# An RWKV-7 layer with a mixture of experts on one core: matmuls that nobody reads, and placing tables of their own for the first and the last chunks

## The reference

```python
x = x + attn(layernorm(x))          # RWKV-7 time mixing with 16 heads of 8, then a squared-ReLU FFN
x = x + ffn(layernorm(x))           # router, top-1 of 4 experts 128 -> 512 (gelu), 512 -> 128, layernorm

def step(state, inp):               # inside attn: 512 steps, each needs the one before
    r_t, d_t, k_t, v_t, a_t, b_t = inp
    sa = einsum('bhij,bhj->bhi', state, a_t)
    state = state * d_t[:, :, None, :] + sa[..., None] * b_t[:, :, None, :] + v_t[..., None] * k_t[:, :, None, :]
    return (state, einsum('bhij,bhj->bhi', state, r_t))
```

## Time and profile before

| | |
|---|---|
| median of the runs | 1217.21 us |
| profiled execution, its own time | 1216.56 us |
| its span in the trace | 1214.7 us |
| mean granted TensorE clock | 0.931 of 2.4 GHz |
| PE busy | 1043.4 us, 86% |
| PEld busy | 566.0 us, 47% |
| DVE busy | 890.9 us, 73% |
| ACT busy | 668.6 us, 55% |
| POOL busy | 629.7 us, 52% |
| first scan step (L843) | 50.86 us |
| last scan step | 1129.38 us |

### The profile page before, as it was taken

The page is one execution under the profiler, slowest core; times in us unless marked ns, Lnnn a source line. Parts: engine busy times, 40 slices in busy tenths (PEclk is TensorE's granted clock), DMA queues, the critical chain, the costliest instruction groups (busy, mean ns, idle before and its releaser), DMA issues.

```text
span 1214.7 us, 17920 instructions
## 1 busy us (share of the span) xinstructions
PE 1043.4 (86%) x5395; PEld 566.0 (47%) x5395; DVE 890.9 (73%) x2283; ACT 668.6 (55%) x1093; POOL 629.7 (52%) x885
## 2 busy tenths in 40 slices
PE   3666689989898989989898989999798989888866
PEld 2343354455454455455454555455454545454432
DVE  4567777887878787877878787887878787876220
ACT  2634464847475565747475665847475565734331
POOL 0346565565555565555555565555555565555100
PEclk8869899999898999989998999999998999989778
DMA  3101011111111121101111121111111121100110
GB/s 123 27 9 32 21 35 27 27 36 35 44 23 48 27 53 28 35 27 35 44 25 49 25 52 28 34 29 36 44 25 47 27 53 27 38 7 22 31 26 17
DMA packets 62759, 41.88 MB, mean 34 GB/s; under 512 B 7100, under 2 KB 56252, under 8 KB 62536
## 3 DMA queue, kind: packets, MB, share of 16 engines
q1 hardware_dynamic: 62664, 40.74, 13.7%
HBM read 11.35 MB, written 4.19 MB: 13 GB/s over the span
## 4 chain that ended last, share of the span: by engine, by line
PE 58%; DVE 14%; ACT 13%; issue 7%; DMA 4%; SPq 3%; ACTq 0%; DVEq 0%
PE fin_a L514 9%; PE fin_b L514 9%; PE sa_ps L359 9%; PE pre_a L298 6%; PE mid_ps L468 5%; PE fin_b L523 3%; DVE state L857 3%; SPq L262 3%; DMA rs_f<-row_ers 3%; PE mid_ps L298 3%; DVE upd L853 3%; PE vb_ps L338 3%; ACT hid L718 2%; DVE s_a L843 2%; ACT L548 2%
## 5 line engine op out<-in xcount | busy, mean ns | idle before, releaser
L1030 POOL TENSOR_TENSOR plus_kv<-state,kv 128x128 f32<-128x128 f32 x512 | 284.7, 556 | 418.5 <-DVE state L857 393.3
L359 PEld LDWEIGHTS sa_ps<-s_a,con 128*128 128x128 f32 x1024 | 183.6, 201 | 307.2 <-DVE s_a L843 230.3
L359 PE MATMUL sa_ps<-s_a,con 128*128 128x128 f32 x1024 | 237.5, 316 | 76.0 <-DVE s_a L843 75.9
L853 DVE TENSOR_TENSOR upd<-sa_ps,b_t 128x128 f32<-128x128 f32 x512 | 147.8, 289 | 169.5 <-PE sa_ps L359 164.8
L1022 POOL TENSOR_TENSOR s_r<-state,r_t 128x256 f32<-128x256 f32 x256 | 219.1, 856 | 1.3 <-DVE state L857 1.3
L857 DVE TENSOR_TENSOR state<-upd,plus_kv 128x128 f32<-128x128 f32 x512 | 175.2, 342 | 18.0
L843 DVE TENSOR_TENSOR s_a<-state,a_t 128x128 f32<-128x128 f32 x512 | 149.4, 292 | 18.5
L548 ACT ACT_TABLE_LOAD x101 | 129.6, 1283 | 1.8
L514 PE MATMUL fin_b<-h_e,mat 128*128 128x512 f32 x256 | 128.2, 616 | 0.8 <-ACT pick L733 0.8
L514 PE MATMUL fin_a<-h_e,mat 128*128 128x512 f32 x256 | 122.1, 593 | 0.0
L830 DVE TENSOR_TENSOR kv<-vb_ps,k_t 128x512 f32<-128x512 f32 x128 | 87.5, 684 | 0.3 <-issue 0.2
(11 more groups left out here) (197 smaller groups left out, 1733.9 us busy)
## 6 DMA issues: line engine op xcount, KB each, us to landing
rs_p<-row_rs SPq DMA_DIRECT2D x128, 64.0 KB, 2.1
x_in<-xT SPq DMA_DIRECT2D x16, 256.0 KB, 3.1
rs_p<-row_rk SPq DMA_DIRECT2D x64, 64.0 KB, 2.4
x_res<-xT SPq DMA_DIRECT2D x16, 256.0 KB, 2.9
rs_m<-row_frs SPq DMA_DIRECT2D x64, 64.0 KB, 2.1
rs_f<-row_ers SPq DMA_DIRECT2D x64, 64.0 KB, 2.1
rs_f<-row_lrs SPq DMA_DIRECT2D x64, 64.0 KB, 2.1
outT<-res SPq DMA_DIRECT2D x16, 256.0 KB, 2.3
```

The lines of the kernel that those rows point to most:

```text
L359: mm(sa_ps[:, 0:STATE], k("sum8"), s_a[:], start=True, stop=True).then_inc(s["sa"], 1)
L853: tt(ib(upd[:]), ib(sa_ps[:, 0:STATE]), over_i(b_t[c.slot][:, t * B:(t + 1) * B]), ALU.mult).then_inc(s["upd"], 1)
L1030: tt(plus_kv[:, (t % 2) * STATE:(t % 2 + 1) * STATE], st(t), kv[:, at:at + STATE], ALU.add).then_inc(s["plus_kv"], 1)
```

## The change

PE gets matmuls that nobody reads. They multiply 256 columns of the constants (128x256, f32) by the weights that the scan uses, and write columns 256 to 511 of the bank `sa_ps`, of which the scan uses only the first 128. Their slots are the list `keep`. Each first waits until DVE has formed `upd` of the scan step in which it stands, so that it never writes while DVE reads the bank. In iteration -1 there is no wait, and in iterations 16 and 17 the wait is for the last `upd` of all.

There are three tables now: `AT_FIRST` for chunks 0 and 1, with 37 unread matmuls per chunk, `AT_LAST` for chunks 14 and 15 with 26, and `AT` for the other twelve with 10; 246 in all. `AT` itself moves a few operations. All other edits write the sizes of a chunk in a general form (`SIZES`, `c.n`, `c.quarters`, `values_of`); as all 16 sizes are 32, they give the same instructions as before. The scan, the arithmetic and the DMAs are the same.

```diff
+        self.place = AT_FIRST if at < 2 else AT_LAST if at >= CHUNKS - 2 else AT
...
-                if at == AT["c0"]:
+                if at == c.place["c0"]:
...
+                    sums(c, fin_b, 0, "mean32", sq_f, "lj")
+                for n in range(len(c.place["keep"])):
+                    if at == c.place["keep"][n]:
+                        now = c + at // SLOTS
+                        if now.at >= 0:
+                            pe.wait_ge(s["upd"], now.step(at % SLOTS // now.slots + 1 if now.has() else 0))
+                        mm(sa_ps[:, 2 * STATE:4 * STATE], k("sum8"), con[:, 0:2 * STATE], start=True, stop=True, skip_group_check=True)
```

`AT` in full, and of `AT_FIRST` and `AT_LAST` the lines that matter below:

```diff
 AT = {
-    "c0": -32, "j0": -31, "sq0": -31, "rs0": -28, "x_in": -24, "xh0": -23, "x1": -22, "c1": -22, "sq1": -22,
-    "rs1": -22, "j1": -21, "xn": -19, "d_rs0": -18, "xh1": -17, "wa": -16, "dx": -16, "d_rs1": -15,
-    "mix_k": -15, "k": -15, "mix_g": -15, "th_w": -15, "mix_r": -15, "mix_v": -14, "w2": -14, "key": -14,
-    "th_d": -14, "rk": -14, "kks": -13, "val_tm": -11, "v": -11, "k2": -11, "cum": -10, "g1": -10,
-    "d_rk": -10, "p": -8, "val": -8, "k_t": -7, "kk": -7, "val_sb": -6, "r": -6, "kki": -5, "rkb": -5,
-    "rec": -4, "rkb_ps": -4, "r_t": -3, "b_t": -3, "a_t": -2, "g2": -2, "th_g": -1, "bonus": 0, "gate": 0,
-    "bonus_b": 23, "x_res": 34, "gj": 37, "gsq": 37, "grs": 38, "gxh": 39, "gaff": 39, "gg": 39, "wo": 41,
-    "x2": 42, "fsq": 42, "fc": 43, "x2x": 43, "frs": 44, "fj": 45, "xf": 46, "fxh": 48,
-    "hid": (50, 51, 53, 56), "kf": 51, "d_frs": 51, "f1": (52, 52, 53, 54), "f2": (55, 56, 57, 57),
-    "d_ers": 57, "y1": 58, "ec": 58, "ej": 58, "esq": 59, "h": 61, "router": 61, "ers": 62, "best": 62,
-    "onehot": 63, "masks": 63, "h_e": (65, 66, 69, 70), "pick": 66, "pick_sb": 66,
-    "moe": (68, 68, 70, 70, 70, 71, 71, 72, 73, 76, 76, 77, 78, 78, 79, 79), "act": (70, 71, 77, 77),
-    "y1b": 78, "mo": (80, 80, 81, 82), "lsq": 84, "y2": 85, "lrs": 85, "lj": 86, "d_lrs": 86, "store": 89,
-    "lxh": 91, "res": 91,
+    "c0": -32, "j0": -30, "sq0": -30, "rs0": -29, "xh0": -23, "x1": -23, "c1": -22, "sq1": -22, "rs1": -22,
+    "x_in": -21, "j1": -21, "xn": -19, "d_rs0": -17, "xh1": -17, "d_rs1": -17, "wa": -16, "dx": -16,
+    "mix_k": -15, "k": -15, "mix_g": -15, "mix_r": -15, "th_w": -14, "mix_v": -14, "w2": -14, "key": -14,
+    "th_d": -14, "rk": -14, "kks": -13, "val_tm": -11, "v": -11, "k2": -11, "d_rk": -11, "cum": -10,
+    "g1": -10, "p": -8, "val": -8, "k_t": -7, "kk": -6, "val_sb": -6, "r": -6, "kki": -5, "rkb": -5,
+    "keep": (-5, -4, 1, 2, 28, 30, 61, 90, 92, 95), "rec": -4, "rkb_ps": -4, "r_t": -3, "b_t": -3, "a_t": -2,
+    "g2": -2, "th_g": -1, "bonus": 0, "gate": 0, "bonus_b": 23, "gj": 37, "gsq": 37, "grs": 38, "gxh": 39,
+    "gaff": 39, "gg": 39, "wo": 41, "x2": 42, "x_res": 43, "fsq": 43, "fc": 44, "x2x": 44, "frs": 44,
+    "fj": 45, "xf": 46, "fxh": 48, "d_frs": 50, "kf": 51, "hid": (52, 53, 53, 57), "f1": (52, 52, 53, 54),
+    "f2": (55, 56, 57, 57), "d_ers": 57, "y1": 58, "ec": 58, "ej": 58, "esq": 59, "ers": 59, "h": 61,
+    "router": 61, "best": 62, "onehot": 63, "masks": 63, "h_e": (65, 66, 69, 70), "pick": 66, "pick_sb": 66,
+    "moe": (68, 68, 70, 70, 71, 71, 71, 72, 73, 76, 76, 77, 78, 78, 79, 79), "act": (70, 72, 76, 77),
+    "y1b": 75, "mo": (80, 81, 81, 82), "lsq": 84, "y2": 85, "lrs": 85, "d_lrs": 85, "lj": 86, "lxh": 90,
+    "res": 90, "store": 91,
+}
+AT_FIRST = {
+    "c0": -32, "j0": -31, "sq0": -31, "rs0": -30,
+    "keep": (-28, -28, -27, -27, -25, -19, -19, -18, -15, -12, -12, -9, -7, -5, -5, -4, -1, 0, 2, 6, 7, 11, 12, 18, 22, 25, 28, 30, 33, 34, 59, 60, 63, 65, 80, 92, 95),
+    "x1": -26, "xh0": -24, "c1": -23, "sq1": -23, "rs1": -23, "j1": -22, "xn": -22, "x_in": -21, "th_w": -20,
+    "xh1": -18, "d_rs0": -17, "wa": -16, "dx": -16, "mix_k": -15, "k": -15, "mix_g": -15, "mix_r": -15,
...
+AT_LAST = {
...
+    "keep": (-4, -2, 0, 1, 2, 3, 24, 27, 29, 29, 34, 46, 54, 58, 59, 62, 82, 87, 90, 90, 91, 92, 93, 93, 95, 95),
...
+    "ej": 58, "d_ers": 61, "h": 62, "router": 62, "esq": 63, "best": 63, "ers": 64, "onehot": 64,
+    "h_e": (64, 65, 67, 69), "masks": 67, "pick": 68, "pick_sb": 68,
+    "moe": (69, 70, 70, 71, 71, 72, 74, 74, 77, 77, 80, 80, 80, 80, 81, 81), "act": (73, 74, 78, 79),
+    "y1b": 77, "mo": (81, 81, 81, 82), "lsq": 81, "lrs": 85, "d_lrs": 85, "y2": 86, "lj": 86, "lxh": 90,
...
```

More of the change, by code:

```diff
@@ new lines @@
+    "router": 61, "best": 62, "onehot": 63, "masks": 63, "h_e": (65, 66, 69, 70), "pick": 66, "pick_sb": 66,
[8 more added lines that the diff above has]
+    "xh1": -18, "d_rs0": -17, "wa": -16, "dx": -16, "mix_k": -15, "k": -15, "mix_g": -15, "mix_r": -15,
+    "key": -15, "mix_v": -14, "w2": -14, "th_d": -14, "rk": -13, "kks": -13, "val_tm": -12, "v": -12,
+    "d_rs1": -11, "k2": -11, "d_rk": -11, "p": -11, "cum": -10, "g1": -10, "val": -9, "k_t": -7, "kk": -7,
+    "val_sb": -7, "r": -7, "kki": -5, "rkb": -4, "rec": -4, "rkb_ps": -4, "r_t": -3, "b_t": -3, "a_t": -2,
+    "g2": -2, "th_g": -1, "bonus": 0, "gate": 0, "bonus_b": 24, "gj": 37, "x_res": 38, "gsq": 38, "grs": 38,
[3 rows of a table added]
+    "d_ers": 62, "best": 62, "onehot": 63, "masks": 63, "h_e": (66, 66, 69, 70), "pick": 66, "pick_sb": 66,
+    "moe": (68, 69, 70, 70, 70, 70, 71, 72, 73, 73, 74, 77, 78, 78, 79, 79), "act": (72, 72, 76, 78),
+    "y1b": 79, "mo": (80, 81, 81, 83), "lsq": 82, "lj": 84, "y2": 85, "d_lrs": 86, "lrs": 87, "lxh": 90,
+    "res": 90, "store": 91,
+}
@@ L75, with __init__, step, state @@
 class Chunk:
-    def __init__(self, base, off):
-        self.base, self.off = base, off
-        self.slot = off % RING
+    def __init__(self, at):
+        self.at, self.slot = at, at % RING
+        self.steps = SIZES[at] if 0 <= at < CHUNKS else SLOTS
+        self.slots = SLOTS // self.steps
+        self.start = sum(SIZES[:max(at, 0)])
+        self.n, self.quarters = self.steps * B, self.steps // QUARTER
+        self.tiles = self.n // C
+        self.place = AT_FIRST if at < 2 else AT_LAST if at >= CHUNKS - 2 else AT
+        self.cols = slice(self.start * B, self.start * B + self.n)
     def __add__(self, n):
-        return Chunk(self.base, self.off + n)
+        return Chunk(self.at + n)
     def has(self, back=0):
-        return not isinstance(self.base, int) or 0 <= self.off - back < CHUNKS
+        return 0 <= self.at - back < CHUNKS
     def count(self, done=1, per=1):
[L91 to L104, removed]
+        return self.at * per + done
+    def step(self, done):
+        return self.start + done
+    def state(self, done):
+        return self.start + self.at + done
+    def quarter(self, done, per=1):
+        return self.start // QUARTER * per + done
 def build(nc, xT, mats, vecs, consts, b1_in, out):
@@ L249, in over_channels @@
             def over_channels(c, name, to, free=(), heads=None):
[L251 to L255, removed]
+                for n, back in free:
+                    if c.has(-back):
+                        sp.wait_ge(s[n], (c + back).count())
+                sp.wait_ge(s["row_" + name], c.count())
@@ L330, in spread @@
             def spread(c, q, half):
-                pe.wait_ge(s["val_rep"], c.count(2 * q + half + 1, 2 * QUARTERS))
-                before = c.count(2 * q + half, 2 * QUARTERS)
-                if not (isinstance(before, int) and before == 0):
+                pe.wait_ge(s["val_rep"], c.quarter(2 * q + half + 1, 2))
+                before = c.quarter(2 * q + half, 2)
+                if before > 0:
                     pe.wait_ge(s["kv"], before)
@@ L504, in work @@
                     for e in range(E):
[L505 removed]
+                        if at == c.place["moe"][j * E + e]:
                             if j == 0:
@@ L556, in replicate @@
                 act.wait_ge(s["val_tm"], c.count())
-                before = c.count(2 * q + half - 1, 2 * QUARTERS)
-                if not isinstance(before, int) or before > 0:
+                before = c.quarter(2 * q + half - 1, 2)
+                if before > 0:
                     act.wait_ge(s["vb"], before)
```

559 lines of the change are left out of this document (287 added, 272 removed), and 3 rows, old and new, of the table AT_FIRST.

## The result

The changed kernel takes 1226.2 us (median of 4 runs, 1223.7 to 1228.4) against 1216.8 us, the median of the kernel before with a fourth run added: ratio 1.0072, 95% interval 1.0054 to 1.0091. The forecast was 1206 us in a range of 1191 to 1217 us, with 0.11 on slower. The profiled execution took 1223.73 us, the fastest of the four, with a span of 1221.9 us.

What follows compares the result with a forecast made beforehand. Bound by the circle s_a, scan matmul, upd, state, which PE enters through its queue and a clock falling in light steps. 1216.56 - 2.6 (middle) - 3.4 (start) - 5.3 (end) = 1205.3 us profiled, forecast 1206 us, range 1191 to 1217.

Steps and rivals of the forecast that it cites:

- the one on chunks 0 and 1: Start: 5.8 us of clock won less unread matmuls' cost saves 2.5 us, iteration -1 0.9 us; 3.4 us together.
- the doubles: Two unread matmuls in one step, in eight steps of chunk 0: 8 x 0.3 = 2.4 us lost.
- The end: Chunk 15 and the serial tail: 3.0 us up to y1, 0.8 router, 1.5 experts; 5.3 us saved (2 to 8).
- The middle: Middle chunks: 12.2 us won by the clock, less 4.2, 3.0 and 2.4 us of costs; 2.6 us saved.
- Steps 31, 0 and 1: Light steps around chunk borders, slow at half clock before: predicted at 1.9, 1.6 and 1.5 us in every chunk.
- Step 2 "0.35 us late": Transposes, j0, an unread matmul and pick in step 2 make PE 0.35 us late, 12 times: 4.2 us.
- `rec` behind `ers`: On ACT, ers ahead of rec starts rec 1.42 us later, delaying GpSimd's rkb: 0.25 us, 12 times, 3.0 us.
- Rival 2: Slower: rec behind ers on ACT between steps 27 and 28 costs up to 1.42 us per chunk; 1220 us, chance 0.09.
- cover of step 28 gone: Sign against the forecast: step 28 at 2 us or more; its three unread matmuls, unhidden, cost 0.9 us per chunk.
- Rival 1: All cover holds: doubles hide behind DVE, ACT order costs nothing, last experts at full clock; 1190 us, chance 0.16.
- Rival 3: The clock still falls: the middle's 12.2 us are not won, the costs stay; 1218 us, chance 0.09.
- Rival 4: The ends bring nothing: doubles and order eat the 8.7 us there; 1215 us, chance 0.09.

Runs made afterwards that it cites:

- f1: The changed kernel with AT_FIRST's real work at AT's places, its 37 unread matmuls kept: 1214.8 us, 0.9973 of the kernel before.
- e4: The changed kernel with lj in AT_FIRST back from slot 84 to 86 and mo to (80, 81, 81, 82): 1224.0 us, ratio 1.0047.
- g2: Kernel before's places, AT's ten unread matmuls per chunk, AT_FIRST's list up to slot 31 for chunks 0 and 1: 1201.9 us, ratio 0.9870.
- e3: All real work at the places of the kernel before, all 246 unread matmuls where the change has them: 1211.7 us, ratio 0.9942.
- f4: Kernel before's places, AT's ten unread matmuls in every chunk, AT_FIRST's 17 before the scan for chunk 0 alone: 1205.2 us, ratio 0.9899.
- f2: The changed kernel with AT in place of AT_LAST, unread list too: 1222.0 us, 1.0026 of the kernel before.
- f3: The changed kernel with AT for all 16 chunks and only ers back from slot 59 to 62: 1207.2 us, 0.9907 of the kernel before.
- g3: Kernel before's places with only AT's four unread matmuls at slots 28, 30, 61 and 95 per chunk: 1215.5 us, ratio 0.9978.
- g4: Kernel before's places with AT's ten unread matmuls moved 14 slots earlier, into steps 12 to 20: 1322.1 us, ratio 1.0854.

## Why the prediction was wrong

**The step that failed** is the one on chunks 0 and 1. It counted what the unread matmuls cost there ("the doubles ... cost 8 x 0.3 = 2.4 us, three more late steps in chunk 1 0.9 us") and what the clock gives back, and ended at 3.4 us saved for the start. AT_FIRST, though, is a whole table: it also moves the real work of the first two chunks, and these slots run up to iteration 3. I costed none of these moves and took chunks 2 and 3 for middle chunks. They cost some 12 us (f1), in three parts of 3.5 to 4.6 us; in the first of them `lj` waits in PE's queue ahead of a scan matmul (e4). In the profile: +2.6 us up to the start of chunk 2 and +8.3 us in chunks 2 and 3, where the forecast had -3.4 and -0.4. With that alone put right the forecast is 1206 + 12 = 1218 us.

**The lists were priced too low as well.** The forecast has the unread matmuls save 2.5 us in chunks 0 and 1. On the old places and at best (g2) these two take 129.2 us, 129.8 before: chunk 0 wins 3.0 us and chunk 1 gets 2.4 us longer, where 0.9 us was counted. The 5.8 us of clock to be won there were not all won: steps 7 to 10 and 15 to 17 of chunk 1 run at the half clock, in whole or in part, in the changed kernel too. Up to the end of chunk 3 the profile of f1, which has the list without the places, is 1.3 us shorter than before where the forecast had 3.8. These 2.5 us and the 3.3 us of the end below bring the sum to 1224 us. The profiled execution took 1223.7 us; the median of the runs lies 2.5 us above it, inside their scatter of 4.7 us.

**The end** was 5.3 us saved and came out at 2.0: 3.0 us were for the earlier end of the scan and the work up to `y1`, the rest for the clock. The clock part held (the end 3.8 us shorter, clock 0.98 instead of 0.82). The mechanism of the earlier scan is there too: steps 29 and 30 of chunk 15, with `h` and the router, take 3.26 us together instead of 6.35. But the other steps of the chunk gave 2.3 us of it back, so its scan ended 0.8 us earlier against its start and not 3, and chunk 14 took 2.6 us more. The prediction priced the unread matmuls there at 0.6 and 0.9 us; AT_LAST's list alone costs 4 to 5 us (e3 against f4), and AT_LAST's other places were not weighed (step 20 of chunks 13 and 14 takes 2.7 us, 1.65 in f2).

**The middle** came out right in total and partly for other reasons. Chunks 4 to 12 took 1.8 us less than before; the forecast's 2.6 us over 12 chunks is 2.0 us for these nine. By its parts:
- Steps 31, 0 and 1 at 1.92, 1.59 and 1.52 us in chunks 4 to 12 (but for one step 1 of 1.63), and the clock at 1.00: as predicted.
- Step 2 "0.35 us late": the interval from `s_a` 3 to 4 is indeed 0.41 us longer (1.93 against 1.52), but the one behind it is 0.31 us shorter (1.52 against 1.83). A cost in a step is not a cost of the chunk. 0.1 us stays of 0.35.
- `rec` behind `ers`: `rkb` starts 58.5 us into the chunk, 58.3 predicted, 56.8 before; it costs 0.33 us per chunk (f3), 0.25 predicted. Rival 2 had the mechanism right, and its "decides where GpSimd's `rkb` holds s_a 28" is what the trace shows; its price of 1.42 us was not reached. What offsets it is not mainly `h` and its DMA, as the prediction had it: step 28 costs 0.99 us, the hold-up of `state` in step 27 goes and gives 0.52 us back, and the step with `h` only 0.13 us.
- Step 28 at 2.5 us was to show "cover of step 28 gone". The sign appeared, its reading was wrong: in f3 three unread matmuls are hidden, as the step's own working said.
- "0.9 or 1.0 of full in the middle" is read too smoothly: seven middle slices of the earlier trace rows show 8. No term of the sum rests on it.

**The rivals.** Rival 1 (all cover holds) is out by the time. Rival 3 (the clock still falls) is out by the clock of 1.00 from chunk 2 on; by g3 and g4 it does fall when unread matmuls are too few or in full steps. Before the fall at 314 us, which the earlier trace rows shows, TensorE's longest idle stretch was 1.30 us, ahead of the router:

```profile
311.98 1.05 PE L483 MATMUL fin_a<-mat,h 128*128 128x4 f32 x8 [1.30 <-DVE h L955]
```

So the trace stays in disagreement with the Trainium skill's "TensorE: Matmul & The Clock Gate", section "Why this matters for your kernels", which asks only for no long gap between bursts.

Rival 4 (the ends bring nothing) pointed to the right place and the wrong size: it gave the ends 0 us; with chunks 2 and 3, which AT_FIRST reaches, they lost 9 us (2.6 + 8.3 - 2.0). The range ended at 1217 us because no case in it had the ends cost anything.

**What the idea is worth.** With the real work left where it was, unread matmuls alone bring 1.3% (g2). Of the changed kernel's 24 us above that, AT_FIRST's places are some 12, AT_LAST with its list 4 and `ers` 4 (0.33 us in the 12 chunks of AT); the remaining 4 us or so are AT's other places and AT_FIRST's list beyond chunk 0, which no run sizes one by one.
